# Weighting the attention values for two key tiles at a time in a one-core adaLN, attention and soft-MoE block

## What is computed

```
mod = silu(c) @ wmod, cut into sa, ca, ga, sb, cb, gb    (ga, gb kept away from zero)
h = layernorm(x) * (1 + ca) + sa
q, k, v = rope(h Wq^T), rope(h Wk^T), h Wv^T             16 heads of width 16
attn = softmax(causal(q k^T / sqrt(16)))
x = x + ga * ((attn v) Wo^T)
h = layernorm(x) * (1 + cb) + sb
x = x + gb * soft_moe(h)                                 8 experts, 128 slots each, hidden 1024
```

## Time and profile before

| | us |
|---|---|
| median of three runs | 3474.62 (3473.63 to 3474.74) |
| the profiled execution | 3468.5 |
| its span | 3466.7 |
| mean granted TensorE clock | 0.965 |
| attention of the first batch, first score unit to last copy | about 149 to 608 |
| TensorE busy in the span | 3148.6 (91%) |
| VectorE busy | 2254.7 (65%) |
| ScalarE busy | 1848.3 (53%) |
| share of TensorE in the chain that ended last | 71% |

### The profile page before, as it was taken

How to read it: one execution, slowest core, us unless ns; L and a number is a source line. 1 busy time by engine, 2 the same in 40 slices (tenths; PEclk the granted TensorE clock), 3 DMA queues, 4 the chain that set the end, 5 groups by cost and what they waited for, 6 DMA issues and landing times.

```text
span 3466.7 us, 45370 instructions
## 1 busy us (share of the span) xinstructions
PE 3148.6 (91%) x17663; PEld 1541.5 (44%) x17663; DVE 2254.7 (65%) x4309; ACT 1848.3 (53%) x3425; POOL 253.1 (7%) x139
## 2 busy tenths in 40 slices
PE   5799999898899999888989999988997999998999
PEld 2433332547553333353754333334575333333468
DVE  5878884662677788366367788836536877874632
ACT  2366667464236666645515666655641566665560
POOL 3100000110400000011030000000122000001100
PEclk9799999999999999999999999999999999999999
DMA  5222200015412120002542202010353221101042
GB/s 147 71 38 38 38 2 26 25 60 181 137 38 35 23 38 2 31 19 96 169 118 50 38 2 38 1 43 7 128 169 98 38 39 22 18 10 41 0 159 97
DMA packets 123694, 202.01 MB, mean 58 GB/s; under 512 B 10108, under 2 KB 107136, under 8 KB 120372
## 3 DMA queue, kind: packets, MB, share of 16 engines
q1 hardware_dynamic: 110960, 148.71, 13.3%
q10 hardware_dynamic: 12520, 50.40, 7.7%
HBM read 156.14 MB, written 42.16 MB: 57 GB/s over the span
## 4 chain that ended last, share of the span: by engine, by line
PE 71%; DVE 12%; ACT 7%; DMA 3%; issue 3%; POOL 2%; ACTq 1%; SPq 1%; DVEq 0%
PE ps L654 15%; PE ps L634 11%; PE ps L574 9%; PE ps L778 7%; PE ps L587 6%; DVE pm L1188 5%; PE ps L752 5%; ACT R L913 2%; PE ps L794 2%; DMA R<-in_L_ffn_w_dram 2%; PE ps L534 2%; PE ps L804 2%; PE ps L619 1%; PE ps L741 1%; PE ps L638 1%
## 5 line engine op out<-in xcount | busy, mean ns | idle before, releaser
L1188 DVE TENSOR_REDUCE pm<-ps 128x1 f32<-128x512 f32 (+4 forms) x2560 | 1395.2, 603 | 265.9 <-PE ps L574 190.1
L913 ACT ACTIVATE R<-ps 128x512 f32<-128x512 f32 (+1 forms) x2240 | 1190.5, 588 | 612.1 <-PE ps L634 418.7
L634 PE MATMUL ps<-R 99*128 99x512 bf16 (+3 forms) x2560 | 822.7, 354 | 26.8 <-ACT R L913 16.0
L654 PE MATMUL ps<-R 128*17 128x512 f32 (+3 forms) x5120 | 598.9, 541 | 24.5 <-ACT R L902 24.0
L574 PE MATMUL ps<-R 96*128 96x512 bf16 x1536 | 575.2, 385 | 24.7 <-DVE pm L1188 21.7
L634 PEld LDWEIGHTS ps<-R 99*128 99x128 bf16 x2560 | 238.4, 98 | 249.7 <-ACT R L913 139.6
L574 PEld LDWEIGHTS ps<-R 96*128 96x128 bf16 x1536 | 147.3, 97 | 453.1 <-DVE pm L1188 346.2
L778 PE MATMUL ps<-R 128*128 128x512 f32 x512 | 233.6, 615 | 12.2 <-ACT R L1005 12.2
L587 PE MATMUL ps<-R 128*128 128x257 f32 x1024 | 235.3, 385 | 4.1 <-ACT R L861 3.6
L752 PE MATMUL ps<-snT,R 128*128 128x512 f32 x512 | 229.8, 594 | 6.3 <-ACT R L951 6.3
L587 PEld LDWEIGHTS ps<-R 128*128 128x128 f32 x1024 | 196.5, 193 | 41.2 <-issue 12.1
(11 more groups left out here) (154 smaller groups left out, 3357.9 us busy)
## 6 DMA issues: line engine op xcount, KB each, us to landing
R<-in_L_ffn_w_dram SPq DMA_DIRECT2D x64, 1024.0 KB, 7.0
R<-q_parts ACTq DMA_DIRECT2D x12, 768.0 KB
R<-k_parts ACTq DMA_DIRECT2D x12, 768.0 KB
R<-in_L_attn_x_dram SPq DMA_DIRECT2D x16, 512.0 KB, 8.1
q_parts<-R SPq DMA_DIRECT2D x16, 512.0 KB, 3.8
k_parts<-R SPq DMA_DIRECT2D x16, 512.0 KB, 3.4
R<-in_L_attn_x_dram SPq DMA_DIRECT2D x4, 2048.0 KB, 8.4
x_park<-R SPq DMA_DIRECT2D x16, 512.0 KB, 2.6
```

The lines of the kernel that those rows point to most:

```text
L634: last = mm(bank[:, i * w:(i + 1) * w], kst[g % 2][0:BROWS, h0 + i, j * P:(j + 1) * P], qst[g % 2][0:BROWS, h0 + i, (c + 1) * CH - w:(c + ...
L654: last = mm(ps[32 * h:32 * h + VC, 6, CH - w:CH], vall[:, j, HG * g + h, :], Eb[s % ESLOTS][:, h, 0:w], start=j == 0, stop=True, skip_grou ...
L913: A(Eb[s % ESLOTS][:, h0:h0 + n, 0:w], ps[:, u % NST, 0:n * w].rearrange("p (n w) -> p n w", n=n), ACT.Exp, scale=SCALE).then_inc(s_ex, 1)
L1188: mx = lambda o, i: V.tensor_reduce(o, i, AX.X, ALU.max)
```

## The change

The table that places the weightings takes, for step `s`, the last unit of step `s | 1` in place of that of `s`. Steps `s` and `s + 1` (for even `s`) are then both weighed after the third unit behind the later one: two calls of `weigh`, eight strip matmuls in a row. The condition after the loop follows the same rule: before and now it catches a batch's last two steps (widths 256 and 128). The step of width 512 before them, weighed three units before the last score unit until now, comes behind the last one. Buffers, semaphores, their values and all other places in the order stay as they are.

```
-WEIGH_AFTER = after_units(LAST_UNIT, WEIGH_BEHIND)
+WEIGH_AFTER = after_units([LAST_UNIT[s | 1] for s in range(NSTEP)], WEIGH_BEHIND)
...
                 for s in range(NSTEP):
-                    if LAST_UNIT[s] + WEIGH_BEHIND >= SU:
+                    if LAST_UNIT[s | 1] + WEIGH_BEHIND >= SU:
                         weigh(s)
```

## The result

The changed kernel takes 3461.48 us (median of 11 runs, 3457.93 to 3470.28) against 3474.62 us: a ratio of 0.9963, 95% interval 0.9954 to 0.9972. It is faster by 13 us, where 13.6 us slower was forecast; the time lies inside the stated range.

The account below looks back on a forecast made before the run. The prediction took the attention to be bound by TensorE, with VectorE and ScalarE not far behind. Its terms summed to +3.4 us a batch, +13.6 for four, so 3488 us, range 3440 to 3525.

Parts of the forecast that it names:

- chunk starts: 15 bursts with transposes: 0.12 us saving left, 0.25 from the first step's wait for the bank 6 copy; -5.6 us a batch.
- The saving of a join: Two weightings in a row pay the fixed part around them once: 0.22 us a pair, 70 us over 320 pairs.
- Rival 4: Joining isn't free: the second step's eight weight loads stand open, 0.13 us each pair, 42 us more, 3530; chance 0.05.
- The bank waits in long bursts: In eight-unit bursts max units wait for VectorE to free one of three banks: 0.49 us with eight full max units.
- the 31 plain ones: Long bursts without diagonal steps at their end: bank waits exceed the join's saving, +5.5 us a batch.
- The diagonal ones: 11 long bursts ending in the diagonal steps: wait about equals saving, +0.17 us each, +1.9 a batch.
- Rival 1: In the plain long bursts the join's saving beats the bank waits, so faster: 3450, or 3422 without waits; chance 0.27.
- The last chunk: Seven bursts behind the last max unit: eight units take 5.28 us against 2 x 2.38; +3.1 us a batch.
- The bursts of three units: 15 bursts behind the diagonal pair: no bank wait, saving 0.20 us each, -3.0 us a batch.
- VectorE's side work: The negation chain delays reduces by 0.99 us, 15 times a batch; between 0 and +14.9 us, taken as +1.5.
- Rival 3: VectorE's 0.99 us chain lands in bursts with full banks and costs its bound, 14.9 us a batch: 3542; chance 0.12.
- Rival 2: Saving and waits cancel over the whole kernel, within 0.2% (7 us): 3475 us; chance 0.18.

Follow-up runs that it names:

- e6: The changed kernel with reduces over at most 256 of a bank's 512 columns (64 of each 128 on the diagonal), not the block's result: 3334.5 us, ratio 0.9592.
- e5: The kernel before with reduces over at most 256 of a bank's 512 columns (64 of each 128 on the diagonal), not the block's result: 3420.7 us, ratio 0.9844.
- e2: Against the kernel before, all pairs of steps joined except the first of each chunk: 3502.4 us, ratio 1.0082.
- e3: The kernel before with the copy of bank 6 on ScalarE one score unit earlier, no step joined: 3452.26 us, ratio 0.9934.
- e4: The kernel before with the first step of each chunk but the first weighed two score units later, still alone: 3451.0 us, ratio 0.9935.
- e1: Against the kernel before, only the first pair of each chunk but the first joined (15 of 80 pairs in a batch): 3447.53 us, ratio 0.9924.
- e7: Against the kernel before, only the first and the last pair of each chunk joined, all other steps alone: 3433.17 us, ratio 0.9883.

## Why the prediction was wrong

The forecast was a sum of six terms, and no single one turned its sign. The largest miss is the term of the chunk starts.

- **The saving of a join** (0.22 us): right. L655 is 0.20 a pair less busy; e6 against e5 shows the whole of it (0.23 in a long burst). Rival 4 (open loads) is refuted: the next matmul starts 1.84 us behind a pair of full width.
- **The bank waits in long bursts**: the mechanism right, the size nearly: the 31 plain ones sum to +5.45 for +5.5, but with luck in it. Their own loss is +6.5 a batch (e2, at full clock), and the two bursts behind starts take 1.3 back. The diagonal ones are +0.24 each for +0.17. Rival 1, the one on the faster side, put its gain here (its "42 plain long bursts" are the 31 plain and 11 diagonal ones together), and it was not here. e2 shows the loss by itself.
- **The last chunk**: right in kind, +2.5 for +3.1 (the prediction's own 5 x 0.52 + 2 x 0.22 is 3.0); the eight units take 5.20, not 5.28 us.
- **The bursts of three units**: -0.25 each for -0.20.
- **The chunk starts: the step that failed.** "saving 0.12 left. The first step's wait for the copy of bank 6 [...] goes [...]; late next is the same copy at the transposes, some 0.2 us." The mechanism was right, the sizes were not. A quiet start takes 6.53 us before and 6.01 after, or 5.91 for 6.42: -0.52, where -0.37 was forecast. Its parts at the same places: the wait for the copy -0.42 (e3; 0.43 forecast), the late copy at the transposes +0.13 (e4 gets only 0.29 of the 0.42), and the join -0.23 (changed kernel against e4, 6.01 for 6.23). So the join saves its whole 0.22 there, not 0.12: the deduction for bank waits was wrong. Not every start is quiet: the one at units 434 to 441 is 0.58 us longer and that at 504 to 511 0.27, so that by luck the 13 starts at full clock sum to -5.0 by themselves (e1), close to 13 x 0.37 = 4.8. What makes the row -8.2 for -5.6 a batch is what the sum had no term for: -1.6 at three starts from the joins in front of them (e2), and -1.6 in two starts, at units 84 to 91 and 224 to 231, in which the clock differs.
- **VectorE's side work**, +1.5 taken near zero out of a bound of +14.9: nothing was left of it. The 14 bursts with a rows unit moved by -0.8 to +1.2 us each and by +1.4 in sum, about what the other terms have for such bursts. Which of them gain and which lose was not forecast, and no run explains it.
- **The clock**, no term at all: it gives 5 us of the changed kernel's gain, 34 against 29 us lost in the profiled attentions and 126 against 121 over the runs.
- **Base.** The terms are off by 5.0 a batch, 20 us. The profiled executions differ by 8.7 us (3468.5 and 3459.83) where the medians differ by 13.1; the attention accounts for 5.9 of the 8.7. The remaining 7 us between forecast and result are, roughly, these: 3 outside the attention, 4 because the profiled execution of before lay further under its median (6.1) than that of after (1.6).
- Rival 3 fell: its side work left no term. Rival 2 was missed by 6 us. The range held only because it was stretched for rival 1, whose mechanism did not happen. A sum of six terms of both signs, each good to a microsecond a batch, times four, can't carry a sign at +3.4: a chance of 0.55 for slower said too much.

## What to carry to other kernels

Look for the wait that a move removes in passing: here a later first use of one accumulator bank was worth more (e4, -24 us) than the whole batching that the move was for (-13), and one number (the copy a unit earlier, e3) gets -22 with no join at all. Batching a long operation pays where the followers' rings are deep enough for it. Count the ring in time: three banks x 0.60 us are 1.8 us, one step's hold with the latency of the first reduce is 0.99 + 0.43 = 1.42, two steps' 1.84 + 0.43 = 2.27. That is an estimate from these traces, and no run changed the number of banks; but joining only where the maxima don't fill the ring (e7) beat joining everywhere by 28 us. A marked wait of a weight load is a cost only as far as the matmuls behind it start late: measure from the matmul in front to the one behind the group (0.38 us marked, 0.13 lost). And before a difference of 5 to 10 us in 3470 is put down to an edit, compare the granted clock, stretch by stretch.

## What the runs showed of the hardware

Four strips of a float32 matmul, repeated for a second step, run on with no seam: 1.05 us shown for one step, 1.91 for two, 1.49 for three of widths 384, 256 and 128. A weight load that waited 0.38 us for a copy delayed the work behind its transposes by 0.13 us. The granted clock fell to its lower level (0.50) inside the attention in runs of max units in which TensorE waited for VectorE, and in e2 after 1.41 us of idle at one place, where the kernel before idled as long and kept the full clock; at the lower level a pair took 3.05 us instead of 1.91. Between the traces of the kernel before, the changed one, e1 and e2 the time lost so in the attention went from 29 to 44 us.
